# Two gated recurrences: products with sums as scans over pairs of entries, an interleaved input part, seeds two steps ahead, fewer idle matmuls

## What is computed

```python
# _L0_cond2_ref, the GRU; one step
fused = sigmoid(concatenate([x_t, h]) @ w_W + w_b)
hidden_state, output_state = split(fused, 2)
memory_state = x_t @ wx_W + wx_b + hidden_state * (h @ wh_W + wh_b)
h = output_state * h + (1.0 - output_state) * tanh(memory_state)

# _L1_cond2_ref, the LSTM; one step
a = xw_t + prev_h @ Wh                     # xw_t = x_t @ Wx + b
i, f, o, g = sigmoid(a[0]), sigmoid(a[1]), sigmoid(a[2]), tanh(a[3])
next_c = f * prev_c + i * g
next_h = o * tanh(next_c)

# around them
x = x + L0_attn(L0_cond(cond, x));  x = x + L0_ffn(L0_cond2(x, cond))    # the GRU
x = x + L1_attn(L1_cond(cond, x));  x = x + L1_ffn(L1_cond2(x, cond))    # the LSTM
```

## Time and profile before

| | us |
|---|---|
| median of 3 runs (lowest, highest) | 6985.24 (6977.26, 6986.25) |
| profiled execution, its own time | 6983.42 |
| its span, first to last instruction | 6981.6 |
| of it: `gru`'s loop / `lstm`'s loop | about 288 / 306 |

### The profile page before, as it was taken

One profiled execution on the slowest core, in us unless ns is written; L12 is line 12 of the kernel. 1 busy time (PEld: TensorE's weight loads), 2 busy tenths in 40 slices (PEclk: granted clock), 3 DMA queues, 4 the chain that ended last, 5 costly groups with the idle time before them and its releaser, 6 DMA issues. The chain is left out here.

```text
span 6981.6 us, 152684 instructions
## 1 busy us (share of the span) xinstructions
PE 5730.2 (82%) x49639; PEld 3105.1 (44%) x49913; DVE 5765.9 (83%) x11628; ACT 4481.1 (64%) x9795; POOL 2712.0 (39%) x2035
## 2 busy tenths in 40 slices
PE   5888888888888888888888768888888887934989
PEld 3555555555555555555555323333333334522543
DVE  4898999999999999989999789999999994446333
ACT  6888888888888888888888744444444442323322
POOL 3222222222222222222222179999999980000000
PEclk9999999999999999999999889999999998966999
DMA  0000000000000000000000010000000000000000
GB/s 8 2 2 2 2 2 2 2 2 2 2 2 2 2 2 2 2 2 2 2 2 2 20 31 4 4 3 4 4 3 4 4 2 3 4 7 3 0 18 6
DMA packets 14195, 30.48 MB, mean 4 GB/s; under 512 B 3665, under 2 KB 11602, under 8 KB 12434
## 3 DMA queue, kind: packets, MB, share of 16 engines
q1 hardware_dynamic: 13586, 22.47, 1.2%
HBM read 15.12 MB, written 7.34 MB: 3 GB/s over the span
## 5 line engine op out<-in xcount | busy, mean ns | idle before, releaser
L423 ACT ACTIVATE rx_junk<-rx_z 128x384 bf16<-128x384 f32 x2178 | 1371.5, 636 | 0.3
L1079 POOL TENSOR_TENSOR hc<-hh,cg 128x512 f32<-128x512 f32 x1024 | 1277.0, 1267 | 80.8 <-DVE hh L1059 75.3
L1000 ACT ACTIVATE ps_m<-ps_m,aneg 128x508 f32<-128x508 f32 x1024 | 673.6, 658 | 875.9 <-DVE hh L1059 834.3
L1059 DVE TENSOR_TENSOR_SCAN hh<-ps_m,bx 128x512 f32<-128x512 f32 x1024 | 1214.0, 1209 | 13.8 <-POOL bx L1083 13.8
L511 POOL TENSOR_TENSOR rx_z<-rx_z 128x512 f32<-128x512 f32 x256 | 384.8, 1503 | 1950.0 <-ACT rh_z L441 1946.7
L964 PE MATMUL ps_m<-hc,pick 128*128 128x512 f32 x2048 | 1056.0, 599 | 9.8 <-POOL hc L1079 8.5
L648 DVE TENSOR_REDUCE rh_ends<-rh_z 128x4 f32<-128x1536 f32 x512 | 960.3, 1917 | 124.3 <-ACT rh_z L441 124.3
L517 POOL TENSOR_TENSOR rx_z<-rx_z 128x1024 f32<-128x1024 f32 x274 | 656.0, 2395 | 73.4 <-DVE rx_z L612 36.7
L338 PE MATMUL r_ps<-rx_z,negid 128*128 128x256 f32 x2192 | 530.8, 384 | 103.2 <-POOL rx_z L511 90.6
L314 PE MATMUL r_ps<-rh_z,negid 128*128 128x256 f32 x2048 | 498.5, 385 | 111.6 <-ACT r_ps L435 111.6
L342 PE MATMUL r_ps<-rx_z,negid 128*128 128x512 f32 x1096 | 506.7, 605 | 62.2 <-POOL rx_z L517 62.2
(11 more groups left out here) (393 smaller groups left out, 10662.1 us busy)
## 6 DMA issues: line engine op xcount, KB each, us to landing
rows_scratch<-pc SPq DMA_DIRECT2D x48, 128.0 KB
rows<-rows_scratch SPq DMA_DIRECT2D x128, 48.0 KB
ew<-in_e SPq DMA_DIRECT2D x3, 1024.0 KB, 7.6
rh_z<-in_x_dn SPq DMA_DIRECT2D x1, 1024.0 KB, 4.8
xcur<-in_x_dn SPq DMA_DIRECT2D x1, 1024.0 KB, 5.3
out_x<-xcur SPq DMA_DIRECT2D x1, 1024.0 KB, 3.9
qi<-in_f_q SPq DMA_DIRECT2D x1, 384.0 KB, 3.2
xpw<-in_xp_t SPq DMA_DIRECT2D x1, 257.0 KB
```

The source lines that it names most:

```text
L423: e.activation(junk[:, n % JUNK], xz[i][:, :, n, 2:K2].rearrange("p c k -> p k c"), ACT.Copy, accum_out=xsum[:, i, n:n + 1]).then_inc(x_fo ...
L1000: e.activation(da[un % NDA][:, :, 1:T], ps[:, un % 2, :].rearrange("p (n t) -> p n t", n=NG4)[:, :, 1:T], ACT.Exp, scale=aneg[:, 0:1]).the ...
L1059: e.tensor_tensor_scan(hh[un % NBUF][:], da[un % NDA].rearrange("p n t -> p (n t)"), bx[un % NBUF][:], 0.0, ALU.mult, ALU.add).then_inc(sc ...
L1079: e.tensor_tensor(hc[un % NHC][:], hh[un % NBUF][:], cg[:], ALU.mult).then_inc(weighted, 1)
```

## The change

In `gru`, two pairs of VectorE instructions (product, then sum) become one scan each. A scan runs along a row of entries: state = a[k] * state + b[k]. With entries in pairs, a = 0 in the first of a pair loads b, and the second gives a product with a sum. `cand` is the scan of (0, hidden part + bias) over (reset, input part); `state` is the scan of (0, 1 - upd) over (tanh, h * upd). So tiles have pairs as their last index: reset is written by ScalarE into `cand_in[t, :, 0]` beside the input part, tanh into `blend[..., 0]`, the hidden product into every second word of PSUM on top of a seeded bias, and h is `state[:, :, 1]`, at a fixed address. The seeds are written two steps ahead, behind the state's scan, along with a bias seed and a copy of the state to `gh`. The idle matmuls of a step go from 6 to 3, and in `lstm` from 6 to 5. In `lstm`, ig and c become one scan, with f * c written beside tanh(g).

```diff
-WARM = 6
+GRU_WARM = 3
+LSTM_WARM = 5
@@ gru, PE
-                e.wait_ge(warm, 2)
+                e.wait_ge(warm, 9)
...
-                        e.wait_ge(vec, t * KV + V0)
-                        h = gh[:, bass.ds(t, 1), :].rearrange("p a n -> p (a n)")
+                        e.wait_ge(vec, t * KV + V0 - 3)
+                        h = state[:, :, 1]
-                        e.matmul(ps[:, at + 2, 0:N], gwh[:], h, start=True, stop=True).then_inc(prod, 1)
+                        e.matmul(ps[:, at + 2, 0:2 * N].rearrange("p (n two) -> p n two", two=2)[:, :, 1], gwh[:], h,
+                                 start=False, stop=True, skip_group_check=True).then_inc(prod, 1)
@@ gru, ScalarE
-                        e.activation(reset[:], ps[:, at, 0:N], ACT.Sigmoid).then_inc(act, 1)
+                        e.activation(cand_in[:, bass.ds(t, 1), :, 0].rearrange("p a n -> p (a n)"), ps[:, at, 0:N], ACT.Sigmoid).then_inc(act, 1)
...
-                        e.wait_ge(vec, t * KV + V0 + 2)
-                        e.activation(th[:], r2[:], ACT.Tanh).then_inc(act, 1)
+                        e.wait_ge(vec, t * KV + V0 + 1)
+                        e.activation(blend[:, :, 0], cand[:, :, 1], ACT.Tanh).then_inc(act, 1)
@@ gru, VectorE, before the loop
+                for at in (0, 3):
+                    seed_gates(at // 3, at)
+                    seed_bias(at, warm)
+                e.memset(upd[:], 0.0).then_inc(vec, 2)
+                e.wait_ge(vec, V0)
+                e.memset(cand[:], 0.0).then_inc(warm, 1)
@@ gru, VectorE, a step
-                        e.scalar_tensor_tensor(out=r1[:], in0=ps[:, at + 2, 0:N], scalar=gb[:, 3:4], in1=reset[:],
-                                               op0=ALU.add, op1=ALU.mult).then_inc(vec, 1)
-                        e.wait_ge(vec, t * KV + V0 + 1)
-                        e.tensor_tensor(r2[:], r1[:], at_t(gxt[:, 2], t), ALU.add).then_inc(vec, 1)
-                        seed(t + 1, 3 - at)
+                        e.tensor_tensor_scan(flat(cand[:]), ps[:, at + 2, 0:2 * N],
+                                             cand_in[:, bass.ds(t, 1)].rearrange("p a n two -> p (a n two)"),
+                                             0.0, ALU.mult, ALU.add).then_inc(vec, 1)
                         e.wait_ge(act, t * KA + 2)
-                        e.tensor_tensor(old[:], at_t(gh, t), upd[:], ALU.mult).then_inc(vec, 1)
+                        e.tensor_tensor(blend[:, :, 1], state[:, :, 1], upd[:], ALU.mult).then_inc(vec, 1)
                         e.wait_ge(act, t * KA + 4)
-                        e.tensor_tensor(r4[:], new[:], th[:], ALU.mult).then_inc(vec, 1)
-                        e.wait_ge(vec, t * KV + V0 + 5)
-                        e.tensor_tensor(at_t(gh, t + 1), r4[:], old[:], ALU.add).then_inc(vec, 1)
+                        e.wait_ge(vec, t * KV + V0 + 2)
+                        e.tensor_tensor_scan(flat(state[:]), flat(keep[:]), flat(blend[:]), 0.0, ALU.mult, ALU.add).then_inc(vec, 1)
+                        seed_gates(t + 2, at)
+                        seed_bias(at, vec)
+                        e.wait_ge(vec, t * KV + V0 + 3)
+                        e.tensor_copy(gh[:, bass.ds(t + 1, 1)].rearrange("p a n -> p (a n)"), state[:, :, 1]).then_inc(vec, 1)
@@ lstm, VectorE, a step
-                        e.tensor_tensor(ig[:], keeps[:, 0, :], gg[:], ALU.mult).then_inc(vec, 1)
-                        e.wait_ge(vec, t * KV + V0 + 3)
-                        e.tensor_tensor(cc[:], fc[:], ig[:], ALU.add).then_inc(vec, 1)
+                        e.wait_ge(vec, t * KV + V0 + 1)
+                        e.tensor_tensor_scan(flat(cell[:]), flat(keeps[:, 0]), flat(terms[:]), 0.0, ALU.mult, ALU.add).then_inc(vec, 1)
```

More of the change, by code:

```diff
@@ L1149, in gru @@
         gw = sb("gw", [128, 2, 2 * D]); gwx = sb("gwx", [128, D]); gwh = sb("gwh", [128, D]); gb = sb("gb", [128, 4])
-        gx = sb("gx", [128, 3, COLS + N])
-        reset = sb("reset", [128, N]); upd = sb("upd", [128, N]); new = sb("new", [128, N])
-        r1 = sb("r1", [128, N]); r2 = sb("r2", [128, N]); th = sb("th", [128, N]); old = sb("old", [128, N]); r4 = sb("r4", [128, N])
+        gx = sb("gx", [128, 2, COLS + 2 * N])
+        cand_in = sb("gcand_in", [128, T, N, 2])
+        upd = sb("upd", [128, N]); keep = sb("gkeep", [128, N, 2]); blend = sb("gblend", [128, N, 2])
+        cand = sb("gcand", [128, N, 2]); state = sb("gstate", [128, N, 2]); hbias = sb("ghbias", [128, N, 2])
         idle = sb("g_idle", [128, 512], BF16)
@@ L1156, in gru @@
         KV, KA, KP = 6, 4, 3
-        V0 = 2
+        V0 = 4
+        flat = lambda x: x.rearrange("p n two -> p (n two)")
         with nc.Block() as blk:
@@ L1211, in _, with seed_gates, seed_bias @@
                 e.memset(gx[:, :, COLS:], 0.0).then_inc(warm, 1)
-                e.wait_ge(moved, 12)
[L1213 to L1220, removed]
+                e.memset(keep[:], 0.0).then_inc(warm, 1)
+                e.memset(hbias[:], 0.0).then_inc(warm, 1)
+                e.wait_ge(warm, 4)
+                e.wait_ge(loaded, 80)
+                e.tensor_copy(hbias[:, :, 1], gb[:, 3:4].to_broadcast([128, N])).then_inc(warm, 1)
+                e.tensor_copy(state[:, :, 1], gh[:, 0, :]).then_inc(warm, 1)
+                e.wait_ge(warm, 6)
+                e.wait_ge(moved, 12)
+                def seed_gates(t, at):
+                    e.tensor_copy(ps[:, at:at + 2, 0:N], gx[:].rearrange("p q (t n) -> p q t n", n=N)[:, :, bass.ds(t, 1), :]
+                                  .rearrange("p q a n -> p q (a n)"))\
+                        .then_inc(vec, 1)
+                def seed_bias(at, done):
+                    e.tensor_copy(ps[:, at + 2, 0:2 * N], flat(hbias[:])).then_inc(done, 1)
+                for at in (0, 3):
[4 more added lines that the diff above has]
+                e.memset(cand[:], 0.0).then_inc(warm, 1)
                 with e.Fori(0, T // STEPS) as block:
@@ L1247, in lstm @@
         gx = sb("lgx", [128, 4, COLS + N])
-        keeps = sb("lkeeps", [128, 2, N]); out_ = sb("lout", [128, N]); gg = sb("lgg", [128, N]); cc = sb("lcc", [128, N])
-        ig = sb("lig", [128, N]); fc = sb("lfc", [128, N]); tc_ = sb("ltc", [128, N])
+        keeps = sb("lkeeps", [128, 2, N, 2]); out_ = sb("lout", [128, N]); cell = sb("lcell", [128, N, 2])
+        terms = sb("lterms", [128, N, 2]); tc_ = sb("ltc", [128, N])
+        flat = lambda x: x.rearrange("p n two -> p (n two)")
         idle = sb("l_idle", [128, 512], BF16)
@@ L1270, in _ @@
                 e.wait_ge(moved, 16)
-                e.wait_ge(warm, 2)
+                e.wait_ge(warm, 3)
                 for _ in range(16):
@@ L1284, in _ @@
                                 i.then_inc(prod, 1)
-                        for _ in range(WARM):
+                        for _ in range(LSTM_WARM):
                             e.matmul(ps[:, 7, :], idle[:, 0:D], idle[:], start=True, stop=True)
@@ L1309, in _ @@
                 e.memset(gx[:, :, COLS:], 0.0).then_inc(warm, 1)
+                e.memset(keeps[:], 0.0).then_inc(warm, 1)
                 e.wait_ge(moved, 16)
-                e.memset(cc[:], 0.0).then_inc(vec, 1)
+                e.memset(cell[:], 0.0).then_inc(vec, 1)
                 gxt = gx[:].rearrange("p (b q) (t n) -> p t b q n", n=N, q=2)
```

22 lines of the change are left out of this document (12 added, 10 removed).

## The result

| | us | ratio to the kernel before |
|---|---|---|
| before, median | 6985.7 | 1 |
| after, median of 4 runs | 7155.3 (7150.9 to 7161.8) | 1.0246 [1.0230, 1.0262] |
| after, span of the profiled execution | 7149.1 | |

The changed kernel is 2.5% slower. The prediction was 6928 us with a range from 6902 to 6966 and a chance of 0.06 for slower: wrong in sign, and 227 us off.

The account below looks back on a forecast made before the run. No engine was taken as the bound, but the length of one step's chain. GRU steps -57.6, heads +8.1, start +1, LSTM -7.7 and -1 gave -57 us against 6983.4, so 6926; forecast 6928, range 6902 to 6966.

Parts of the forecast that it names:

- What the step costs at full clock: GRU step's chain, interval by interval: 1.77 against 2.22 us, over 128 steps -57.6 us.
- LSTM's loop against before, six idle: LSTM: tanh(g) to tanh of the cell 0.58 against 0.64, -7.7 us; five idle matmuls instead of six, -1 us.
- The scan's price: GRU scans of 32 entries: 0.227 us from the line through longer scans, taken as 0.23.
- C: Rival: dearer scans, 0.33 us instead of 0.23, three scans in 128 steps, +38 us: 6966; chance 8%.
- D: Rival: cheaper waits, ScalarE's register step hidden (-13 us), scans at 0.17 (-23 us): 6892; chance 6%.
- The round's head: GRU rounds: table load behind the product's wait, its 1.28 us wholly on the path eight times, +8.1 us.
- the 1 us at the start: Once: PE's 16 idle matmuls wait for nine initial VectorE instructions, +1 us.
- What I cost at nothing: GRU step: seeds, copy to `gh`, h * upd and fewer idle matmuls, all taken as covered, no time added.
- Rival B: GRU loop's clock halves with half its idle matmuls gone: +0.62 a step, +79 us, 7007, slower; chance 6%.
- Rival A: GRU's hidden product into every second PSUM word takes twice as long: +47 us, 6975, counted as same; chance 5%.

Follow-up runs that it names:

- a_head_g5_l6: Kernel after with 5 idle matmuls in the GRU, 6 in the LSTM, and an early sigmoid putting the table load ahead of the wait: 6922.8 us, 0.9911.
- a_fill_g5_l6: Kernel after with 5 idle matmuls in the GRU, 6 in the LSTM, and 6 more in each GRU round's first step: 6932.1 us, 0.9923.
- b_l5: Kernel before with 5 idle matmuls instead of 6 in the LSTM, nothing else changed: 7138.9 us, 1.0224.
- b_g3: Kernel before with 3 idle matmuls instead of 6 in the GRU, nothing else changed: 7034.7 us, 1.0072.
- experiment 1: Kernel after with 6 idle matmuls a step in both loops, 6943.8 us, or with 6 in the LSTM alone, 7001.7 us.
- a_g3_l6: Kernel after with 6 idle matmuls in the LSTM, the GRU still with 3: 7001.7 us, 1.0028.
- experiment 5: The run b_g3: kernel before with 3 idle matmuls instead of 6 in the GRU: 7034.7 us, 1.0072.
- a_g5_l6: Kernel after with 5 idle matmuls in the GRU and 6 in the LSTM, table load still behind the wait: 7105.2 us, 1.0175.
- experiment 6: The run a_head_g5_l5_burst: a_head_g5_l6 with 5 idle matmuls in the LSTM, 16 more in each round's first step: 6966.3 us, 0.9980.
- a_head_g5_l5_burst: a_head_g5_l6 with 5 idle matmuls in the LSTM and 16 more there in the first step of each round: 6966.3 us, 0.9980.

## Why the prediction was wrong, and where it was right

**What the step costs at full clock: right.** Where the clock held, nearly every term can be read. One GRU step of a_head_g5_l6:

```profile
5902.23 0.30 PEld L1187 LDWEIGHTS ps_g<-gstate,gw 128*128 128x128 f32 x2 [0.93 <-DVE gstate L1256]
5902.76 0.18 ACT L1209 ACTIVATE gcand_in<-ps_g 128x16 f32 x1 [0.93 <-PE ps_g L1187]
5903.11 0.23 DVE L1249 TENSOR_TENSOR_SCAN gcand<-ps_g,gcand_in 128x32 f32<-128x32 f32 x1 [0.58 <-PE ps_g L1190]
5903.37 0.22 ACT L1214 ACTIVATE gblend<-gcand 128x16 f32<-128x16 f32 x1
5903.72 0.22 DVE L1256 TENSOR_TENSOR_SCAN gstate<-gkeep,gblend 128x32 f32<-128x32 f32 x1 [0.21 <-ACT gblend L1214]
5903.99 0.19 PEld L1187 LDWEIGHTS ps_g<-gstate,gw 128*128 128x128 f32 x1 [0.33 <-DVE gstate L1256]
```

| piece | predicted | measured |
|---|---|---|
| weight load to reset's sigmoid | 0.53 | 0.53 |
| sigmoid to the first scan | 0.34 | 0.35 |
| first scan to tanh | 0.27 | 0.26 |
| tanh to the state scan | 0.35 | 0.35 |
| state scan to the next weight load | 0.28 | 0.27 |
| step | 1.77 | 1.76 |
| LSTM, tanh(g) to tanh of the cell (kernel after) | 0.58 | 0.56 |
| LSTM's loop against before, six idle | -7.7 - 1 | -8.6 |

The scan's price, worked out from the earlier trace rows as 0.227 us, is this in the kernel after (group by line and form, busy us, mean ns | idle before; the first scan has 224 ns):

```profile
L1254 DVE TENSOR_TENSOR_SCAN gstate<-gkeep,gblend 128x32 f32<-128x32 f32 x128 | 28.8, 225 | 14.9 <-ACT gblend L1212 3.0
```

So C and D fall. The round's head was sized rightly too: in a_fill_g5_l6, whose table loads are as late as in the kernel after, the first step of a round takes 3.02 us from weight load to weight load (3.13 in the first round) instead of 1.76, some 10.2 us in eight rounds; before, it takes 2.54 (2.35 in the first round) instead of 2.22, some 2.4. The difference is 7.8 us, against 8.1. All in all a_fill_g5_l6 came to 6932 where the sum said 6928. The one term that no run isolates is the 1 us at the start. (Half of D's gain below 6928 would be 6910; the range went on to 6902.)

**The step that failed: "What I cost at nothing", the fewer idle matmuls.** The prediction looked at them only as work that ends late (GRU) or that covers a shorter step (LSTM), and asked what time they take. It didn't ask what they hold. They hold the clock, in both loops, and each loop loses it for itself: b_l5 loses 155 us by the LSTM's cut alone, b_g3 50 by the GRU's. The text named the cover of each hidden edit, as it should; for the idle matmuls of the LSTM, "five end 0.22 earlier, which covers the shorter step", it stopped at the step's length and put a gain of 1 us on it, where 140 were lost.

Two smaller readings went into it. "Six end 2.15 after the weight load and would hold up a step of 1.77" takes the end that the profile models for the last matmul as the time at which the next weight load can start. With six, the measured step is 1.88 (experiment 1): the next weight load, 5902.71, starts 0.38 us ahead of that end, 5901.63 + 1.46 = 5903.09. So keeping six would have cost 1.88 - 1.77 = 0.11 a step, and five, with a step of 1.76, nothing. And in the LSTM nothing needed cutting: with six the loop already had its whole -8.6 us.

**Rival B: the right mechanism, a size that came out partly by luck, too small a chance, and one loop short.** B described what happened to the GRU: 7007 was its time, and a_g3_l6, in which the GRU alone is at half clock, took 7001.7. But its +0.62 a step isn't the hidden product alone: that comes 0.42 later (experiment 5), and in the kernel after, the step that follows PE's wait at a head takes 2.27 us from weight load to weight load (5900.69 to 5902.96), 0.51 over 1.76. The other steps there take 2.37 us, set by PE's string with its three idle matmuls, to which B gave no price; with five it is 3.23 (a_g5_l6).

What B lacked was the LSTM, where the cut looked too small to be weighed. And its chance of 6% leaned on a stretch that was too short: the 7 us in the mamba stage with PE busy for 4.88 us kept 1.00, but in the kernel before the clock fell to half 7 us behind them, at 4494.0, for 3.4 us, after a wait of PE of 1.51 us and in the middle of one of 1.16:

```profile
4490.00:4498.00 8.00, 5.05 (x12) 1.96 (x12) 8.00 (x9) 3.81 (x7) 7.00 (x6) 0.79 0.00 0
```

If the LSTM's measured loss of 140 us is put in place of the gain of 8.7 that B's 7007 contains, the two loops give 7156; the measured median is 7155.

The Trainium skill (TensorE: Matmul & The Clock Gate, "HAM oscillation — how this bites in real kernels") explains such drops by gaps between bursts of matmuls, in which PE waits for data. The GRU's first head with its 1.52 us is such a gap, if a shorter one than the page's waits for transfers, and a_fill_g5_l6, which fills it, keeps 1.00. The LSTM doesn't fit this: b_l5 lost its clock with PE waiting 0.24 us a step, the kernel after with 0.17, and neither had a longer gap in the loop before the fall.

**Rival A: not there.** The hidden product into every second PSUM word took 0.38 us at full clock (5823.69 above) beside 0.37 before, and the first scan, which waits for it, starts 0.88 us after the weight load (a_head_g5_l6) where the sum without such a price said 0.87. The Trainium skill's rule on patterns that aren't contiguous (SBUF — State Buffer, "Door 1: The DMA port swizzle (why `[64,N]` ≈ `[32,N]`)") shows no effect on these 16 columns, and the measurement decides.

**What stays open.** Which measure of PE's activity the chip goes by these runs don't tell. The number of idle matmuls by itself isn't it: five a step keep the clock in the GRU's step of 1.76 us (a_head_g5_l6) and lose it in the LSTM's of 2.31 (kernel after). In the LSTM no run changes the number while PE's wait stays the same, so there the two aren't separated. Nor do the runs tell why the moment of the fall varies so much: 6 us into the loop with three idle matmuls in the GRU, 205 with four in one run, 36 in the LSTM of the kernel after and 8 in b_l5. That half clock can go on for 400 us with PE hardly standing still, and that with the same bursts the full clock was lost 11 us into the loop and later held for 147 (experiment 6), is measured and not explained.

## What to carry to other kernels

Filler matmuls in a loop of small products are not idle time to be trimmed by their duration: before one is removed, ask what it holds, and price the loss of the clock for every loop that it is removed from, however small the cut. Read the granted clock of the loop first, of each loop apart, and only then the intervals of a step. When a wait moves onto a register instruction ahead of a ScalarE table load, the load moves behind the wait; one early activation that depends on nothing puts it back.

## What was not expected of the hardware

- One idle matmul less, 0.22 us (1.46 for six, 1.24 for five), in a step of 2.4 us took 155 us from a loop of 305 (b_l5), with PE waiting 0.24 us a step.
- Half clock lasted although PE hardly stood still: it was busy for 393.9 of 400 us in the LSTM's loop after, and the granted clock stayed at 0.50, that is 1.2 GHz. Both bursts of sixteen more idle matmuls that met half clock ended at full clock, 2.4 GHz (a_head_g5_l5_burst).
- At half clock more filler is dearer: the GRU's loop took 308 us with three idle matmuls and 410 with five, the same loop 229 with five at full clock.
